# Where the second input of the transformer layer is made: 49 blocks split over the score stage and the message stage

## What is computed

```python
x = _layernorm(x + L1(x))                        # "second input": the residual input of layer 2
x_norm = _layernorm(x, g1, be1)
q, k, v = x_norm @ Wq + bq, x_norm @ Wk + bk, x_norm @ Wv + bv
scores = (q[src] * k[tgt]).sum_per_head / 4 + (curv @ Wc + bc)     # score stage, per edge
probs  = softmax of scores over the edges with the same tgt        # softmax stage
out    = zeros.at[src].add(probs * v[tgt]) @ Wo + bo               # message stage
x = x + out                                                       # transformer stage, per node
return x + relu(_layernorm(x) @ W1 + b1) @ W2 + b2
```

## Time and profile before

| what | value |
|---|---|
| time, median of 3 runs | 5331.2 us (5328.56 to 5365.31) |
| the profiled execution | 5342.85 us, its span 5341.1 us |
| score stage, POOL's first gather to the first DVE instruction of the softmax stage | 2603.1 to 3149.7 |
| message stage, POOL's first gather to the first DMA of the transformer stage | 3217.0 to 3651.5 |
| DVE busy over the span | 71% |

### The profile page before, as it was taken

One profiled execution on the slowest core, in us unless ns is written; L12 is line 12 of the kernel. 1 busy time (PEld: TensorE's weight loads), 2 busy tenths in 40 slices (PEclk: granted clock), 3 DMA queues, 4 the chain that ended last, 5 costly groups with the idle time before them and its releaser, 6 DMA issues. The chain is left out here.

```text
span 5341.1 us, 70175 instructions
## 1 busy us (share of the span) xinstructions
PE 3358.2 (63%) x19808; PEld 2649.4 (50%) x19808; DVE 3813.6 (71%) x10966; ACT 2396.5 (45%) x5571; POOL 3005.8 (56%) x2733
## 2 busy tenths in 40 slices
PE   6888855288612367643277644556999993774453
PEld 1455554277601255533266633334777763764443
DVE  8877777399834467622377777886899874877997
ACT  6444400299700156532123213544666662325776
POOL 7777577245577433257777726765776556107400
PEclk9989977699855689865588867878999996996666
DMA  5666588299757778832367527883555545876654
GB/s 208 180 190 198 167 304 289 92 299 314 242 187 260 249 237 276 275 107 73 96 212 259 186 61 224 279 277 118 182 192 187 178 142 161 264 218 227 232 213 155
DMA packets 684358, 1095.92 MB, mean 205 GB/s; under 512 B 108888, under 2 KB 451979, under 8 KB 677722
## 3 DMA queue, kind: packets, MB, share of 16 engines
q1 hardware_dynamic: 580772, 908.27, 51.9%
q0 software_dynamic: 103200, 183.16, 11.4%
HBM read 664.33 MB, written 439.19 MB: 207 GB/s over the span
## 5 line engine op out<-in xcount | busy, mean ns | idle before, releaser
L2242 PE MATMUL ro_end<-vals,end_mask 128*2 128x128 f32 x1600 | 240.5, 315 | 373.2 <-DVE vals L2106 276.4
L2368 POOL DMA_INDIRECT sc_rows<-layer,node_idx x400 | 391.5, 979 | 124.4 <-issue 121.6
L719 POOL DMA_INDIRECT agg<-late_agg_sent,d_last x200 | 223.2, 1116 | 324.5 <-issue 295.8
L2242 PEld LDWEIGHTS ro_end<-vals,end_mask 128*2 128x2 f32 x1600 | 147.3, 96 | 457.2 <-DVE vals L2106 287.6
L2974 ACT ACTIVATE tf_hidden<-tf_h_ps,pre_b 128x512 f32<-128x512 f32 x392 | 268.8, 687 | 227.0 <-PE tf_h_ps L3014 217.0
L2268 PE MATMUL ro_acc<-vals,ro_mask 128*126 128x128 f32 x1600 | 248.3, 320 | 187.3 <-ACT ro_square L2200 140.5
L1601 POOL DMA_INDIRECT cap_own<-layer,w_own x200 | 205.7, 1028 | 278.9 <-SPq L1581 227.2
L3026 PE MATMUL tf_o_ps<-pre_w,tf_hidden 128*128 128x128 f32 (+1 forms) x3136 | 358.0, 275 | 0.0
L3026 PEld LDWEIGHTS tf_o_ps<-pre_w,tf_hidden 128*128 128x128 f32 (+1 forms) x3136 | 353.9, 192 | 0.5 <-issue 0.5
L3014 PE MATMUL tf_h_ps<-tf_x_t,pre_w 128*128 128x512 f32 x784 | 348.2, 597 | 9.5 <-ACT tf_hidden L2974 8.3
L213 POOL DMA_INDIRECT x_src<-in_x_dram,node_idx x200 | 295.6, 1478 | 81.7 <-issue 59.4
(11 more groups left out here) (502 smaller groups left out, 11021.1 us busy)
## 6 DMA issues: line engine op xcount, KB each, us to landing
ro_mask<-masks SPq DMA_DIRECT2D x100, 504.0 KB, 4.9
layer<-zeros SPq DMA_DIRECT2D x96, 512.0 KB
si_both<-layer SPq DMA_DIRECT2D x48, 1024.0 KB, 6.1
ro_far<-far SPq DMA_DIRECT2D x75, 512.0 KB, 6.1
ro_both<-both SPq DMA_DIRECT2D x75, 512.0 KB, 6.0
agg<-zeros SPq DMA_DIRECT2D x48, 512.0 KB
mom_x<-in_x_dram SPq DMA_DIRECT2D x48, 512.0 KB, 9.8
mom_agg<-agg SPq DMA_DIRECT2D x48, 512.0 KB, 8.1
```

What stands on the lines that cost most here:

```text
L719: pool.indirect_dma_start(out=self.dest, out_offset=bass.IndirectOffsetOnAxis(ap=self.order.last_idx[:, t:t + 1], axis=0), in_=self.sent[: ...
L2242: mm = nc.tensor.matmul(end_ps[0:2, j, :], k.end_mask[:, t, :], k.vals[:, t, :], start=True, stop=True, skip_group_check=True)
L2368: nc.gpsimd.indirect_dma_start(out=rows[:, g % SC, c * GT + j, :], out_offset=None, in_=k.layer1, in_offset=bass.IndirectOffsetOnAxis(ap=k ...
```

## The change

Two `SecondInput` objects instead of one. The first makes blocks 0 to 24 in the score stage, the second blocks 25 to 48 in the message stage. Each works in every second group only (`paced`), with lags that count groups: SP `load` 0 and `store` 5, DVE `negate` 4 and `add` 2, ACT `root` 2 and `normalise` 4. So block i of a part is loaded in SP's iteration 2i, added in DVE's iteration 2i + 2, normalised in ACT's iteration 2i + 4 and stored in SP's iteration 2i + 5. The tile `xin` goes: the sum is written into `x2` and normalised in place, and what the sum waits for is now the landing of the store that last read the slot, where before `normalise` waited for it. The stages still stand behind those of the host stage.

```diff
-def scores_phase(k, o, ends):
+def scores_phase(k, o, ends, beside):
...
-                run((load, 0), (put, 4), (lambda g, i, u, p: ends.sync(g), 0))
+                run((load, 0), (put, 4), (lambda g, i, u, p: ends.sync(g), 0),
+                    *alone(beside.sync_stages))
                 ends.close_sync()
+                beside.close_sync(sp)
...
-                run((normalise, 1), (score, 3), (add, 0), (lambda g, i, u, p: ends.vector(g), 0))
+                run((normalise, 1), (score, 3), (add, 0), (lambda g, i, u, p: ends.vector(g), 0),
+                    *alone(beside.vector_stages))
...
                 run((values, 3), (copy, 1), (lambda g, i, u, p: norm.square_root(act, g, u, p), 0),
-                    (lambda g, i, u, p: ends.scalar(g), 0))
+                    (lambda g, i, u, p: ends.scalar(g), 0), *alone(beside.scalar_stages))
...
+SB = 25
...
-        self.sync_stages = (self.load, 0), (self.store, 4)
-        self.vector_stages = (self.negate, 2), (self.add, 1)
-        self.scalar_stages = (self.root, 1), (self.normalise, 2)
-        self.tensor_stages = ()
+        self.sync_stages = self.paced((self.load, 0), (self.store, 5))
+        self.vector_stages = self.paced((self.negate, 4), (self.add, 2))
+        self.scalar_stages = self.paced((self.root, 2), (self.normalise, 4))
+
+    def paced(self, *stages):
+
+        def every_other(stage):
+            return lambda g: g % 2 == 0 and g // 2 < self.count and stage(g // 2, self.first + g // 2)
+        return tuple((every_other(stage), lag) for stage, lag in stages)
...
-        if n >= 2:
-            dve.wait_ge(s["x2_made"], n - 1)
-        dve.tensor_tensor(self.xin[0:p, u, :, :], self.both[0:p, u, :, 0:D], self.both[0:p, u, :, D:2 * D],
+        if i >= 2:
+            dve.wait_ge(s[f"x2_put{u}"], i // 2 * 16)
+        dve.tensor_tensor(self.x2[0:p, u, :, :], self.both[0:p, b, :, 0:D], self.both[0:p, b, :, D:2 * D],
                           ALU.add).then_inc(s["added"], 1)
...
-        self.norm.normalise_on_act(act, n, u, p, self.x2[:, u, :, :], self.xin[:, u, :, :]).then_inc(s["x2_made"], 1)
+    def normalise(self, i, n):
+        u, p = i % 2, tail(n)
+        self.norm.normalise_on_act(self.k.nc.scalar, i, u, p, self.x2[:, u, :, :], self.x2[:, u, :, :])\
+            .then_inc(self.s["x2_made"], 1)
...
-            scores_phase(k, by_dst, ends)
+            with ExitStack() as second:
+                scores_phase(k, by_dst, ends, SecondInput(k, second, 0, SB))
...
-                second_input = SecondInput(k, second)
+                second_input = SecondInput(k, second, SB, NG + 1 - SB)
```

## The result

The changed kernel takes 5415.0 us in the median (5404.7 to 5430.6, 5 runs), the kernel before 5334.5 beside it: ratio 1.0147, 95% interval 1.0119 to 1.0175. It is 1.5% slower, 81 us. The forecast had +50 us and 5382, with 5325 to 5435 as the range.

A forecast was written before the change was run, and what follows sets the result against it. The prediction took POOL's gathers to bound the score stage and DVE's list, with POOL waiting, the message stage. Adding +43 and +7 us to the 5331.2 median gave about 5382 us, range 5325 to 5435.

The forecast's parts named there:

- the sum of +50: Whole kernel: score stage +43 and message stage +7 us, giving about 5382 us on the median, +0.95%.
- Score stage, +43 forecast: Score stage: DVE stalls 1.5 us for ACT's late query copy, pairs take 21.8 us, softmax starts 43 us later.
- Rival (a): Score stage keeps POOL's pace, ACT's late copy absorbed: +13 instead of +43, 5352 us; chance 0.17 shared with another rival.
- In the score stage POOL should wait for `sc_xin`: Score stage: profile sign that POOL waits for DVE's sum of gathered rows, with sums 21.8 us apart by pairs.
- The traffic at nothing: Score stage: 25 x 1.5 MB more DMA traffic costs nothing, since gathers at 1034 ns still give 21.3 us a pair.
- Message stage, +7 forecast: Message stage: half the blocks leave, but SP's store holds the row of ids; +7 us, bounds -11 and +70.
- 11.9 + L: Message stage: length of a pair of groups in us, taken as 16.9, bounds 16.1 and 19.8.
- L: Message stage: landing time of the row of ids after issue, taken as 5.0 us, bounds 4.2 and 7.9.
- +2: Message stage: the last block, of 106 partitions, makes the row of ids behind it late, costing 2 us.
- (c): Message stage is freed and POOL becomes the bound: -70 us there, 5304 us with the score stage's +43; chance 0.11.
- (b): Message stage: ids land as late as now, 7.9 us after issue, 64 us more, 5446 us; chance 0.12.
- The result in place of the sum: Both stages: the sum waits for the store of two blocks before, costing nothing while it lands within 9 us.

The follow-up runs named there:

- e2: Changed kernel with ACT's eight `normalise` instructions of the score stage moved one group back, behind the odd group's copies: 5421.4 us, ratio 1.0153.
- e5: Changed kernel with the message stage's store one group later and the score stage's `normalise` ahead of the host's square root on ACT: 5315.5 us, ratio 0.9957.
- e12: Changed kernel with each two-input sum of the score stage and of the blocks cut into four instructions: 5422.2 us, ratio 1.0153.
- e7: Changed kernel with all block work in the score stage but only two blocks loaded and stored in its loop: pair 21.7 us, sums span 542 us.
- e11: e4 with the score stage's sum of the gathered rows cut into four instructions: score stage 548.6 us, one run.
- e4: Changed kernel with the score stage's block loads and stores kept but DVE's and ACT's work for them left out: 5383.3 us, score stage 564.5, one run.
- e1: Changed kernel with SP's store of a block one group later in the message stage alone (lag 6 for 5): 5338.3 us, ratio 0.9997.

## Why the prediction was right, and where it was off

**Direction and range.** 5415 lies in the range 5325 to 5435. The chances for slower and for no change were nearly equal (0.43, 0.49), because the sum of +50 stood at the 1% line; measured were +81, over that line, which was the less likely of the two. Much of why 5415 lies inside is that the range is 110 us wide; the account of the two stages is the better test, and it follows.

**Score stage, +43 forecast, +40.9 measured: right in its main terms.** The stall in the odd group was put at 1.5 us and is 1.46. The pair was put at 21.8 and is 21.7. The 22 pairs with the work in `ends` were put at 487 us and take 485. Two smaller terms were off and nearly cancel: group 4's sum comes 55.2 us into the stage instead of 52.1, and the last block takes 7.4 us behind the last score instead of 10.1. The order on ACT as the cause is shown by e2 (the stall goes where `normalise` goes), e5 (less stall, pair 21.1) and e12 (the pair does not shrink when POOL is freed). Rival (a), POOL's pace kept, falls.

**Score stage, two steps that were wrong but cost nothing here.** "In the score stage POOL should wait for `sc_xin`": it never does. DVE's sums hold it about 0.5 us three times a pair: 16 gathers at 1047 + 305 ns are 21.6 us, level with DVE's 21.7. That the two limits coincide fits holds that set POOL's phase anew by the sum that caused them; e12, where the holds are gone, shows which of the two is the limit. And the price of the gathers was wrong in kind: I took the message stage's 1034 ns in the earlier trace rows as what traffic does to a gather. In e7 they take 1050 without the traffic, in e11 976 with it. The 1047 was inside my bounds (979 to 1129 ns) by luck of the rows, not by reasoning. The traffic at nothing holds in the changed kernel (e7 has the same pair), but not alone (e4, +17.9 us).

**Message stage, +7 forecast, +30.1 measured: the mechanism was right, two terms were mis-sized.** The pair was 11.9 + L. Measured: 17.9 with L at about 5.9, so the rest is 12.0. L was taken as 5.0, "near the lower row of its own stage", and each us of it is worth 22 us: 0.9 x 22 = 20 of the 23 us that were missing. The row that I leaned on was the minimum of 5.2 in the earlier trace rows and the 4.2 of a stage with less beside it. The forecast asked only what is ahead of the row, "the 512 KB store alone". For that 5.0 is a fair size: such rows of e1 land in 4.1 to 5.1. What it left out is the 1 MB load that SP issues 0.44 us behind the row, and with it they land in 4.8 to 6.5. The second term is the last block. The row beside its load landed 23.2 us after its issue, and the pair around it took 24.5 us instead of 17.8: 6.7 where the forecast had "+2". With that, 20 + 5 us, the stage is accounted for: group 4's `negate` came 38.6 us into the stage (39 forecast), and what follows group 48's `negate` took 27.9 (28 forecast).

The Trainium skill's fit (DMA: Bandwidth & Descriptors, section Anatomy of one DMA), which had given L near 3.3, is stated there for DMAs issued from GpSimd, and these come from SP. The measured 5.9 is far above it, and so are the 4.1 to 5.1 of e1 behind a store alone.

**Rivals.** (c), the message stage freed, did not come in the changed kernel, but its point of decision was the right one: whether the store holds the row of ids. e1 moves just that, and the stage takes 386.3 us, 48 below before. The rival's -70 was too much: POOL's list in e1 takes 355 us from its first gather to its last (3257.1 to 3612.0), where I had counted 333. The rows had it: busy and issue time of the earlier trace rows add up to 206.9 + 56.0 + 72.2 + 19.9 = 355, and with 355 the rival's -70 is -48. (b), L at 7.9, did not come: too large by 2.

**The result in place of the sum** costs nothing that shows: no wait for a store of `x2` stands among DVE's larger waits in the changed kernel, as forecast. That was not tested by itself.

**What stays open.** Stage by stage the profiled executions differ by +71 us where the medians differ by 81; executions differ by 20 us and more in stages whose code is the same (the start of the score stage above), so this isn't settled to better than that. The end of the score stage, where the softmax starts 7.4 us behind the last score instead of 2.5, was in the forecast (the last block's `normalise` and store).

## What to carry to other kernels

When work is taken out of a stage, check the lists of the idle engines for what now stands in front of a load: here one store, one position too early on SP, cost 78 us, more than the 48 that the work removed was worth. When work is put into "slack", ask not only whether it fits but which instruction of which engine it stands ahead of; the same eight ACT instructions made DVE wait 1.5, 2.5 or about 0.4 us a pair in three places (the last is e5: 24.2 us of waits for the query copy against 15.0 before, over 22 pairs). If a latency carries a weight of 22 in the sum, list what is issued right behind it as well as what is ahead, and don't take the best value of its row.

## What the runs showed of the hardware that I had not expected

**A DVE sum of two SBUF tensors holds a gather's issue on POOL.** A gather (indirect DMA, issue 0.95 us) that starts while the 1.22 us sum of 128x1024 runs, with more than about 0.13 us of it left, ends 0.81 to 0.83 us after the sum, whatever its start (ends at 2697.80, 2925.99 and 2782.16 for sums that end at 2696.98, 2925.18 and 2781.35; so do all 71 of the changed kernel's score stage that start in a sum). In the message stages it is 0.81 to 0.86. The exceptions are gathers that start within 0.04 us of the sum's own start, two in the score stages (e4, e5) and more in the message stages: they last 0.95, and the sum takes 1.25 to 1.29. A gather that is already running when the sum starts isn't touched, and a sum that holds a gather takes no longer itself (1.21 to 1.23 us in the three above). Reductions (`sc_dots`), bn_stats and the 0.68 us product with one operand in PSUM (`sc_terms`, 94 gathers over all traces) left the gathers at 0.95. Over a stage the cost is a matter of phase: gathers in the mean of 979, 1016 and 982 ns with the sum at its place, 0.4 and 1.2 us later.

The sum is not the only such instruction, and one kind does more. In the kernel before, a gather that had started 0.34 us before a `TENSOR_SCALAR` with one SBUF tensor was lengthened by it, to 1.55 us:

```profile
2824.53 1.55 POOL L2368 DMA_INDIRECT sc_rows<-layer,node_idx  x1 [0.30 <-issue]
...
2824.87 1.08 DVE L2551 TENSOR_SCALAR ee_edge<-ee_ids 128x1664 f32<-128x1664 f32 x1
```

In the fourteen traces 25 of 26 gathers that were running when this instruction began are lengthened, 24 of them to 1.55 us. One SBUF input instead of two therefore doesn't make an instruction harmless to the gathers.

The Trainium skill (SBUF — State Buffer, section Who interferes with whom) says that a DVE instruction with two SBUF inputs contends with a GpSimd instruction that reads SBUF, because its second input comes through a read interface that the two engines share. The traces agree in so far as the gather, whose index column lies in SBUF, is held for all that is left of the sum. They don't agree with the same section's note that `tensor_tensor` was not seen to stall a DMA issued there: for the indirect DMAs of this kernel it does.

**Traffic that delays nothing directly still cost 18 us** (e4): it shifted when the rows landed, and so where in the gather's issue the sum fell; cutting the sum into four took 16 of the 18 back (e11) at the same traffic.
